# Attention pooling on one Trainium2 core: one activation pair of each tile made by ScalarE alone from two ReLUs, key tiles loaded in four transfers, and another order at the start

## The reference

```
feat = concatenate([qe, k, qe - k, qe * k], axis=-1)      # 2048 x 200 x 512
h = feat @ W1 + b1                                        # ... x 64
h = where(h >= 0, h, alpha[0] * h)
a = (h @ W2 + b2)[..., 0]                                 # 2048 x 200
a = where(mask == 0, NEG, a)
w = softmax(a, axis=-1)
out = einsum('bl,bld->bd', w, k)                          # 2048 x 128
```

## Time and profile before

| | |
|---|---|
| median of 3 runs | 1019.24 us (1017.79 to 1035.44) |
| the profiled execution | 1018.95 us, of which the span from the first to the last instruction is 1017.0 us |
| busy, share of the span | PE 83%, DVE 76%, POOL 65%, ACT 52% |
| mean granted TensorE clock | 0.983 |
| transfers | 222.45 MB, mean 219 GB/s |
| the chain that ended last | PE 40%, DVE 16%, DMA 15%, issue 13%, ACT 8%, SPq 7% |

### The profile page before, as it was taken

The page is one execution under the profiler, slowest core; times in us unless marked ns, Lnnn a source line. Parts: engine busy times, 40 slices in busy tenths (PEclk is TensorE's granted clock), DMA queues, the critical chain, the costliest instruction groups (busy, mean ns, idle before and its releaser), DMA issues.

```text
span 1017.0 us, 55327 instructions
## 1 busy us (share of the span) xinstructions
PE 847.9 (83%) x25216; PEld 559.4 (55%) x25216; DVE 769.4 (76%) x1143; ACT 532.8 (52%) x1281; POOL 656.3 (65%) x401
## 2 busy tenths in 40 slices
PE   0769888988888898889889889888887888888896
PEld 0435555655555565556555556555555555545564
DVE  2879777878788778787787888777886777867771
ACT  0355545655555565555555555555554555545552
POOL 0657666767667676676666667667666667657661
PEclk9899999999999999999998999999999999989999
DMA  8844766667776766786675777766677676667630
GB/s 253 322 148 138 268 204 212 233 201 239 253 236 228 238 206 230 238 270 211 229 231 185 236 266 238 232 223 226 204 242 257 211 230 209 217 225 233 213 103 11
DMA packets 67017, 222.45 MB, mean 219 GB/s; under 512 B 25312, under 2 KB 33504, under 8 KB 66784
## 3 DMA queue, kind: packets, MB, share of 16 engines
q1 hardware_dynamic: 66784, 218.92, 65.0%
HBM read 214.57 MB, written 4.33 MB: 215 GB/s over the span
## 4 chain that ended last, share of the span: by engine, by line
PE 40%; DVE 16%; DMA 15%; issue 13%; ACT 8%; SPq 7%; POOL 0%; DVEq 0%; ACTq 0%; POOLq 0%
PE hP L431 22%; DMA keys<-in_r_k 9%; PE poolP L472 9%; DVE act L348 9%; PE scoreP L460 7%; ACT act L289 6%; DVE keysT L340 5%; DMA probs_scratch<-expd 5%; SPq L160 3%; SPq L211 2%; ACT expd L313 2%; PE poolP L480 1%; DVE neg_max L361 1%; DVE logits L355 1%; DMA w2c<-in_L_rec_W 1%
## 5 line engine op out<-in xcount | busy, mean ns | idle before, releaser
L289 ACT ACTIVATE act<-hP,biast,al 128x200 f32<-128x200 f32 x1024 | 459.5, 515 | 329.6 <-PE hP L431 325.9
L340 DVE STREAM_TRANSPOSE keysT<-keys 128x768 f32<-128x768 f32 (+1 forms) x512 | 510.1, 997 | 60.4 <-DMA keys<-in_r_k 60.3
L431 PE MATMUL hP<-keysT,weff 32*64 32x200 f32 x16384 | 475.5, 344 | 30.3 <-issue 23.5
L232 POOL TENSOR_TENSOR weff<-qX,wp 128x1024 f32<-128x1024 f32 x128 | 244.0, 1906 | 324.3 <-PE hP L431 300.7
L431 PEld LDWEIGHTS hP<-keysT,weff 32*64 32x64 f32 x16384 | 310.2, 133 | 186.2 <-issue 113.1
L348 DVE TENSOR_TENSOR act<-hP,act 128x400 f32<-128x400 f32 x512 | 283.9, 554 | 146.8 <-ACT act L289 143.0
L236 POOL TENSOR_TENSOR weff<-weff,wk 128x1024 f32<-128x1024 f32 x128 | 303.2, 2369 | 10.0
L472 PE MATMUL poolP<-keys,pool_w 128*16 128x128 f32 x6400 | 244.6, 276 | 22.7 <-issue 21.2
L472 PEld LDWEIGHTS poolP<-keys,pool_w 128*16 128x16 f32 x6400 | 173.4, 97 | 98.1 <-issue 93.0
L460 PE MATMUL scoreP<-act,w2win 128*16 128x200 f32 x2048 | 151.3, 341 | 81.3 <-DVE act L348 70.3
L271 POOL TENSOR_TENSOR pool_w<-probs_k,own_b 128x400 f32<-128x400 f32 x128 | 111.3, 870 | 15.7 <-DMA probs_k<-probs_scratch 7.9
(11 more groups left out here) (35 smaller groups left out, 40.9 us busy)
## 6 DMA issues: line engine op xcount, KB each, us to landing
keys<-in_r_k SPq DMA_DIRECT2D x128, 832.0 KB, 5.5
keys<-in_r_k SPq DMA_DIRECT2D x128, 768.0 KB, 5.2
probs_scratch<-expd SPq DMA_DIRECT2D x32, 100.0 KB, 3.7
masks<-in_r_mask SPq DMA_DIRECT2D x128, 12.5 KB
probs_k<-probs_scratch SPq DMA_DIRECT2D x128, 12.5 KB
out_rows<-pooled SPq DMA_DIRECT2D x128, 8.0 KB
keys<-in_r_q SPq DMA_DIRECT2D x4, 256.0 KB, 5.0
act<-in_L_rec_W SPq DMA_DIRECT2D x4, 128.0 KB, 6.1
```

The costliest lines, as they stand in the source:

```text
L232: g_.tensor_tensor(weff[:, n % 2, :, :, :], qX[:, n, :, :].unsqueeze(3).broadcast_to([P, BQ, CD, H]), wp[:].unsqueeze(1).broadcast_to([P, ...
L289: a_.activation(act[:, k, a, :], hP[:, 2 * (p % HSETS) + a % 2, 0:L], ACT.Identity, bias=biast[:, n, k, a:a + 1], scale=al[:]).then_inc(t_ ...
L340: v_.transpose(keysT[:, n % TBUF, j0 * D:j1 * D], keys[:, n % SLOTS, j0 * D:j1 * D]).then_inc(keysT_done, 1)
L431: mm = t_.matmul(hP[H * r:H * r + H, 2 * (p % HSETS) + a % 2, 0:L], weff[QP * a:QP * a + QP, n % 2, w, c, :], kT[QP * a:QP * a + QP, :, c, ...
```

## The change

**ScalarE alone for pair 1 of each tile** (p % 4 = 1, k = 0, the rows a = 2 and 3). ScalarE writes max(h, 0) to `act` and max(-h, 0) to a new tile `act_neg`, with bias and scale of its own: four operations of 128x200 in place of two. VectorE's maximum of this pair is gone. The second layer of half 0 multiplies the first by `w2pos` (W2 times the slope of the positive side) and the second by `w2neg` (W2 times minus that of the negative side), so it has six matmuls in place of four; the two added ones go to the column strips of a = 2 and 3. TensorE waits for `relu_done` where it waited for `act_done` of that pair.

**Keys in four transfers.** `load_keys` issues a tile's keys in four transfers that are cut like the transposes, all at once when the slot is free; the pacing by `keysT_done` is gone, and so is the wait for older keys in the loads of the start. In the steps with n % 4 = 1 the masks stand behind the keys.

**The start.** The six parameter vectors are issued first. VectorE transposes the queries before it folds, has eight small operations more, puts pieces 0 and 1 of tile 0 before the bias and 2 and 3 behind it. TensorE and ScalarE begin the first tile without waiting for the shift, which is waited for before the first second_layer instead; the shift has 24 matmuls for 32.

The core of the diff:

```diff
+RELU = 1
+def by_dve(p):
+    return p - p // PAIRS - (p % PAIRS > RELU)
...
-            def load_part(n, x):
-                at = slice(LOAD_CUT[x] * D, LOAD_CUT[x + 1] * D)
-                sp.dma_start(keys[:, n % SLOTS, at], k_tiles[n][:, at]).then_inc(keys_in[n % SLOTS], 16)
             def load_keys(n):
-                for x in range(LOADS):
-                    load_part(n, x)
+                for x in range(PIECES):
+                    at = slice(CUTS[x] * D, CUTS[x + 1] * D)
+                    sp.dma_start(keys[:, n % SLOTS, at], k_tiles[n][:, at]).then_inc(keys_in[n % SLOTS], 16)
...
             for n in range(1, SLOTS):
-                if n > 2:
-                    sp.wait_ge(keys_in[n - 2], 16 * LOADS)
...
             for n in range(STEPS):
-                def paced_part(x):
-                    if SLOTS <= n + AHEAD < TILES:
-                        behind = PIECES * (n + 1) + 2 + x * PIECES // LOADS
-                        sp.wait_ge(keysT_done, min(behind, PIECES * TILES))
-                        load_part(n + AHEAD, x)
                 if SLOTS <= n + AHEAD < TILES:
                     sp.wait_ge(part_done, n + AHEAD - SLOTS + 1)
-                paced_part(0)
+                    load_keys(n + AHEAD)
...
+                if p % PAIRS == RELU:
+                    ge(act_e, score_done, HALVES * (n - 1) + k + 1)
+                    for a in (2 * pair, 2 * pair + 1):
+                        a_.activation(act[:, k, a, :], hP[:, 2 * (p % HSETS) + a % 2, 0:L], ACT.Relu,
+                                      bias=bias_own[:, n, a % 2:a % 2 + 1]).then_inc(relu_done, 1)
+                        a_.activation(act_neg[:, a % 2, :], hP[:, 2 * (p % HSETS) + a % 2, 0:L], ACT.Relu,
+                                      bias=biast[:, n, k, a:a + 1], scale=-1.0).then_inc(relu_done, 1)
+                    return
...
             def activate(p):
-                if not 0 <= p < PAIRS * TILES:
+                if not 0 <= p < PAIRS * TILES or p % PAIRS == RELU:
                     return
-                dve.wait_ge(t_done, 2 * p + 2)
+                dve.wait_ge(t_done, 2 * by_dve(p) + 2)
...
-                    ge(pe, act_done, p - HSETS + 1)
+                    last = p - HSETS
+                    if last >= 0 and last % PAIRS == RELU:
+                        pe.wait_ge(relu_done, 4 * (last // PAIRS) + 4)
+                    elif last >= 0:
+                        pe.wait_ge(act_done, by_dve(last) + 1)
...
             def second_layer(n, k):
-                pe.wait_ge(act_done, PAIRS * n + 2 * k + 2)
+                pe.wait_ge(act_done, by_dve(PAIRS * n + 2 * k + 2))
+                if k == RELU // 2:
+                    pe.wait_ge(relu_done, 4 * n + 4)
...
+                if k == RELU // 2:
+                    for a in (2 * (RELU % 2), 2 * (RELU % 2) + 1):
+                        mm = t_.matmul(scoreP[QP * a:QP * a + HALF_Q, 0:L],
+                                       w2neg[:, HALF_Q - 2 - 2 * t:2 * HALF_Q - 2 - 2 * t],
+                                       act_neg[:, a % 2, :], start=False, stop=(t == HALVES * GT - 1))
```

More of the change, by code:

```diff
@@ L201, in _ @@
                     load_mask(g + 2)
-                for x in range(1, LOADS // 2 + 1):
-                    paced_part(x)
                 if n % GT == 0 and 0 <= g < GROUPS:
@@ L212, in _ @@
                                      ).then_inc(probs_in[GT * (g % 2) + t], 16)
-                for x in range(LOADS // 2 + 1, LOADS):
-                    paced_part(x)
                 m = n - 1 - LAG
@@ L307, in _ @@
                 scale_pair(PAIRS * n)
+                if n == 0:
+                    act_e.wait_ge(fold, 11)
+                    fill(0)
                 g = n // GT - 1
@@ L397, in _ @@
             v_.tensor_scalar(biast[:], bias[:], al1[:], None, ALU.mult).then_inc(bias_done, 1)
+            dve.wait_ge(bias_done, QUADS + 1)
+            own = (slice(None), slice(None), RELU // 2, slice(2 * (RELU % 2), 2 * (RELU % 2) + 2))
+            v_.tensor_scalar(biast[own], bias[own], -1.0, None, ALU.mult)
+            v_.tensor_copy(bias_own[:], bias[own]).then_inc(bias_done, 1)
+            for piece in range(2, 4):
+                transpose_piece(0, piece)
+            dve.wait_ge(shift_mm, 1)
+            v_.tensor_scalar(nshift[:], scoreP[:, 0:GROUPS], b2c[:], -1.0, ALU.add, ALU.mult).then_inc(fold, 1)
             for piece in range(2):
                 transpose_piece(1, piece)
-            dve.wait_ge(shift_mm, 1)
-            v_.tensor_scalar(nshift[:], scoreP[:, 0:GROUPS], b2c[:], -1.0, ALU.add, ALU.mult).then_inc(fold, 1)
             for n in range(STEPS):
@@ L454, in second_layer @@
             def second_layer(n, k):
-                pe.wait_ge(act_done, PAIRS * n + 2 * k + 2)
+                pe.wait_ge(act_done, by_dve(PAIRS * n + 2 * k + 2))
+                if k == RELU // 2:
+                    pe.wait_ge(relu_done, 4 * n + 4)
+                if n == 0 and k == 0:
+                    pe.wait_ge(fold, 11)
                 if n % GT == 0 and k == 0:
@@ L501, in _ @@
                     for a in range(QUADS):
+                        if 2 * k + a // 2 == RELU:
+                            continue
+                        first = 1 if a // 2 == RELU else 0
                         mm = t_.matmul(scoreP[QP * a:QP * a + HALF_Q, 0:GROUPS],
                                        w2win[:, HALF_Q - 2 - 2 * t:2 * HALF_Q - 2 - 2 * t], by_group[:, s, k, a, :],
[L504 removed]
+                                       start=(t == first), stop=(t == HALVES * GT - 1))
             mm.then_inc(shift_mm, 1)
[L506 to L507 removed]
             for n in range(STEPS):
```

59 lines of the change are left out of this document (35 added, 24 removed).

## The result

The changed kernel takes 1087.92 us (median of 4 runs, 1074.94 to 1100.42), the kernel before 1018.51 in the same runs. The ratio is 1.0675 [1.0518, 1.0833]: 6.75% slower, some 69 us. The forecast was 1033 with a range to 1066; the sign that it held likeliest (slower 0.42, within 2% 0.40) is right, the size is not. The profiled execution of after took 1074.94 us, of which the span is 1073.2, at a mean granted clock of 0.969 for 0.983.

A forecast was written before the change was run, and what follows sets the result against it. No engine is full, so waits bound the kernel: for the softmax, keys and TensorE's instructions. Terms 43.5 + 14 + 0 - 36 + 0 - 7.5 = +14 on 1018.95 gave 1033 us, range 985 to 1066.

The forecast's parts named there:

- two more matmuls a tile: Second layer of half 0: two added matmuls cost 0.34 us a tile, hidden by nothing; +43.5 us, bounds 0 and +59.
- four operations of ScalarE for two: ScalarE's pair 4n+1 reaches TensorE 0.2 us later in three of four steps; +14 us, bounds 0 and +40.
- VectorE's relief: VectorE's 128 maxima of 0.554 us go, but its next transposes wait for ScalarE instead; 0 us.
- keys: Last key part issued 1.9 us earlier, so most of the transposes' 60.3 us stalls vanish; -36 us, bounds 0 and -60.
- dense transfers: Unpaced key bursts may lengthen TensorE's instruction pauses, half-long packets may shorten them; taken as 0, ends -45 and +45.
- the start: Before the first tile: earlier parameters and folding let the first layer begin at 26 for 33.88; -7.5 us, bounds -3 and -10.
- fourth window: Last of four profiled steps: TensorE needed 7.50 us for what took 6.21, read as pauses gathering where transfers are dense.
- Weight loads stand bare: Second layer's strips: four more weight loads a tile at 0.095 us, not overlapped; +49, giving 1082 us; chance 0.05.
- Key tiles land no earlier: Key loads: shorter transfers, or masks and probabilities behind longer bursts, eat the 1.9 us; 1069 us; chance 0.12.
- Pauses go away: TensorE's instruction fetch: half-long packets let the instruction queue in sooner; -45, giving 988 us; chance 0.13.
- VectorE set the pace: VectorE's removed maxima would count throughout; -58, giving 975 us; chance 0.06.
- Pauses grow by half: TensorE's instruction pauses lengthen as nothing spreads the transfers; +22, giving 1055 us; chance 0.12.

The follow-up runs named there:

- no traffic: Changed kernel without the main loop's key transfers (ten slots filled once and reused): 939.98 us with the two added matmuls, 914.92 without; kernel before likewise 923.11.
- loads alone: Kernel before with only the new key loads (four transfers, no pacing, masks behind the keys): ratio 1.0416, median 1066.79 us.
- unpaced in two: Kernel before with only the waits for keysT_done ahead of a tile's two key transfers removed from the main loop: ratio 1.0429.

## Why the prediction was wrong

By its own steps, in its own order. Sizes in us against the kernel before:

| step | forecast | measured | from |
|---|---|---|---|
| two more matmuls a tile | +43.5 | +25 | with and without them, no traffic |
| four operations of ScalarE for two | +14 | -3.5 | groups of 26.91 and 27.02 us, VectorE's relief included |
| VectorE's relief | 0 | not apart | its waits for ScalarE rose from 143 to 321.5 |
| keys | -36 | -34 | second layer's waits, loads alone |
| dense transfers | 0 | +84 | pauses +55.5, busy time +28.9, loads alone |
| the start | -7.5 | -7.2 | first layer's start |

**Dense transfers** is the step that failed, and it outweighs all others. The prediction had the mechanism: it took the 45 us of pauses for TensorE's own instructions fetched behind the keys, noted that nothing would spread the transfers any more, and gave +45 as an end. But it took 0, since no row told which way it would go, and gave even half of that growth 0.12. Where it said "as if each step were like the worst two" the pauses did more than double, 44.7 to 98.0, which is beyond the 70 that it had named as a sign of being wrong; in the loads alone they grew by 55.5. The second half of the failure is that it priced the pauses at their own length only. What comes behind a pause at the lower clock costs about half as much again (28.9 for 55.5), and no term held it.

The row that it read as such a pause showed something else. In the fourth window of the earlier trace rows, 7.50 us of TensorE for what took 6.21, there is no pause: TensorE is busy for all of the window, and the clock is at the lower level from 473.35 to 476.76, right behind the 2.30 us in which TensorE waited for VectorE and the keys. So the row told what the lower clock costs behind a wait of another kind, and nothing on where pauses gather. The pauses' own places and times, in the same trace, would have told that they are waits for packets of instructions.

**Keys** was right in mechanism and size: stalls of 7.9 us for "under 15", a gain of 34.2 us in the loads alone. **Two more matmuls** was over-priced. Its 0.34 us was read from the block of the group step, and there it is right: 0.33, and the block of 12 records lasts 0.87 us for a forecast of 0.88. In the three other steps the block runs into the tail of the pooling and they add 0.17; in the trace of before such a block already took 0.62 to the next first layer (463.10 to 463.72) and not 0.46. The undisturbed odd step is 6.37 us and not 6.8. **Four operations for two** was priced with a duration of another operation, 1.73 us for four; the ReLUs take 1.36. **The start** is as forecast, at the first layer.

Two sums of the prediction don't hold as they stand. Its own range of 1013 to 1053 is said to come from the ends of the first two terms, 0 to 59 and 0 to 40; these give 975 to 1074. And its chances add up to 0.98.

The Trainium skill, "TensorE: Matmul & The Clock Gate", part on packing small matmuls, has weight loads overlap only where the row group differs, on which the rival "Weight loads stand bare" rested. The runs don't bear it out here: two added matmuls whose operands span all 128 rows cost 0.20 us a tile, where that rival had four bare loads at 0.38.

Of the rivals, "Key tiles land no earlier" is out (stalls 7.9), "Pauses go away" and "VectorE set the pace" too, and "Pauses grow by half" had the right cause with less than half of its size: 22 for 84. The rule on transfers of 1 MiB and more, from the Trainium skill, "DMA: Bandwidth & Descriptors", section Bandwidth, made no difference: four transfers of about 0.39 MB and two of about 0.8 MB gave 1.0416 and 1.0429 when both went unpaced. Both sizes lie below that mark, so no run here shows what crossing it does.

**The sum with the measured terms**: 25 - 3.5 - 34 + 84 - 7 = +64.5, beside 69 measured. That it fits this well is partly luck. The terms of the loads come from single profiled executions, in which the loads alone are 50 us slower; by its ratio they are 42 +/- 10.

**What stays open.** That TensorE waits for its packets of instructions is shown by the places and times of the pauses, and that the keys' traffic makes these packets late by the runs without it, in which the same instructions leave 3.6 and 5.4 us. How it does so is not shown: no trace tells when a packet was asked for. The Trainium skill, "DMA: Bandwidth & Descriptors", section Queues, rings and completion order, has each DMA engine go round its queues a packet at a time. If the profile's packets are those packets, halving them should have let the instruction queue in sooner, and it didn't: the pauses are 100.2 us with packets of 6 and 6.5 KB (unpaced in two) and 100.2 with 3 and 3.5 KB (the loads alone). Why is open.

## What to carry to other kernels

In a kernel with a long unrolled program, an engine's own instructions come over the same DMA engines as the data: read "issue" in the middle of a uniform run of instructions as a sign that these come late, check it by the places of the pauses (here one every 254 recorded instructions at most) and the landings of the instruction queue's packets, and find its price by one run without the traffic before touching the loads. A wait that paces transfers isn't waste because the engine behind it stalls: what its stalls cost TensorE (34 us) was less than the pauses that came in their place (55 us, and 29 more at a lower clock). Here a way of loading that cut one kind of wait always lengthened the other. Small edits were priced best without the traffic, where nearly all groups of a trace have the same length.

## What the runs showed of the hardware that was not expected

- A tile of keys issued in one go, 1.48 MB in 5.7 us at 81.5% of the DMA engines' time, let no instruction packet through, and the pause of TensorE that followed was 3.50 us; the longest of any run was 3.9. The instruction queue moves 3.31 MB in all, 1.2% of the engines' time, and TensorE's waits for it are 98 us. The Trainium skill, "Runtime: NRT & Kernel Launch", section Instruction fetch mechanics, calls the crossing of a block of instructions mostly hidden; without key traffic this trace agrees (3.6 us in all), beside it not.
- Without the keys' traffic the changed kernel takes 939.92 and 940.03 us in its two runs; with it, 1074.94 to 1100.42 in four.
- On ScalarE, ReLUs of 128x200 from PSUM with a constant scale start 0.31 us apart. Four scalings with a slope per partition take 1.73 us in a row, some 0.43 each. So size alone doesn't set that engine's pace; which of function and scale does wasn't separated. For the scale: the refill of the score tile, the same function with a constant scale, lasts 0.460 us in the mean where a scaling lasts 0.522, but it doesn't read PSUM.
- Six matmuls of 128 rows on four column strips in one block take TensorE 0.33 us longer than four where the block stands alone, and 0.17 where it follows other matmuls without a gap. A matmul's price depends on what it stands behind.
